# A new instruction order for the second and the steady groups of a graph-convolution kernel

## The reference, cut to what matters

```python
h0 = jnp.maximum(_layernorm(x, axis=-1), 0.0)          # rows of 1024
fv = h0.mean(axis=1)                                   # one value per node
nf = fv / norm(fv);  sim = nf[:, :, None] * nf[:, None, :]
_, idx = jax.lax.top_k(sim, 9);  idx = idx[..., 1:]    # 8 neighbours per node
adj = symmetric 0/1 matrix of them, diagonal 1         # 1024 x 1024 per batch
def _gc(x, adj, W, b):
    h = x @ W.T + b
    return einsum('bij,bjh->bih', adj / deg, h)
h = relu(_gc(h0.T, adj, W, b1));  h = _gc(h, adj, W, b2)
out = x + h.T                                          # W is the 256 x 256 input adj
```

## Time and profile before

| | |
|---|---|
| median of 3 runs | 477.64 us (476.87 to 478.04) |
| profiled execution | 475.69 us |
| its span, first to last instruction | 473.9 us |
| PE busy | 421.5 us (89%) |
| DVE busy | 395.6 us (83%) |
| ACT busy | 307.8 us (65%) |
| POOL busy | 220.9 us (47%) |
| mean granted clock of PE | 0.986 |

### The profile page before, as it was taken

How to read it: one execution, slowest core, us unless ns; L and a number is a source line. 1 busy time by engine, 2 the same in 40 slices (tenths; PEclk the granted TensorE clock), 3 DMA queues, 4 the chain that set the end, 5 groups by cost and what they waited for, 6 DMA issues and landing times.

```text
span 473.9 us, 7615 instructions
## 1 busy us (share of the span) xinstructions
PE 421.5 (89%) x2220; PEld 176.2 (37%) x2220; DVE 395.6 (83%) x682; ACT 307.8 (65%) x657; POOL 220.9 (47%) x937
## 2 busy tenths in 40 slices
PE   0653898999978799899999999899999999999996
PEld 0121343334323344344443443344434444344432
DVE  5999898988897998999899998999899828854463
ACT  2979687989766777667777769667766843014400
POOL 2536656374736435552737454744656253415200
PEclk9995999999999999999999999999999999999999
DMA  8990000159202493065703590078404400341026
GB/s 295 382 410 29 1 0 2 44 223 340 107 0 94 174 326 119 1 262 175 273 3 132 205 355 21 0 268 284 160 0 179 177 2 0 142 160 55 0 94 262
DMA packets 19401, 68.21 MB, mean 144 GB/s; under 512 B 1824, under 2 KB 2464, under 8 KB 19360
## 3 DMA queue, kind: packets, MB, share of 16 engines
q1 hardware_dynamic: 19360, 67.73, 38.2%
HBM read 34.17 MB, written 33.55 MB: 143 GB/s over the span
## 4 chain that ended last, share of the span: by engine, by line
DVE 39%; PE 31%; ACT 11%; issue 9%; POOL 7%; DMA 1%; POOLq 1%; SPq 0%; DVEq 0%; ACTq 0%
PE ps L451 26%; DVE hl L1109 9%; DVE hl L1118 7%; DVE bn L1087 7%; DVE xs L1134 5%; ACT hl L663 4%; ACT hf L654 4%; PE ps L457 3%; ACT hl L675 2%; DVE fv L1150 2%; DVE idx L1158 2%; POOL gat L876 2%; PE pm L506 1%; DMA xs<-x_dram 1%; POOL nw L858 1%
## 5 line engine op out<-in xcount | busy, mean ns | idle before, releaser
L451 PE MATMUL ps<-hl,wh 128*128 128x512 f16 x896 | 268.7, 382 | 20.6 <-DVE wl L1293 11.3
L451 PE MATMUL ps<-hl,wl 128*128 128x512 f16 x448 | 170.5, 381 | 0.0
L451 PEld LDWEIGHTS ps<-hl,wh 128*128 128x128 f16 x896 | 83.9, 99 | 131.4 <-issue 22.0
L654 ACT ACTIVATE hf<-xs,nbias,rstd 128x1024 f32<-128x1024 f32 x64 | 79.2, 1237 | 25.3 <-POOL nbias L862 17.4
L1109 DVE TENSOR_TENSOR hl<-hf,hl 128x1024 f16<-128x1024 f32 x64 | 76.9, 1211 | 15.5 <-ACT hl L663 15.3
L1134 DVE SCALAR_TENSOR_TENSOR xs<-ps,sc,xs 128x1024 f32<-128x1024 f32 (+1 forms) x71 | 78.9, 1137 | 5.9 <-PE ps L457 5.9
L1118 DVE SCALAR_TENSOR_TENSOR hl<-ps,hl 128x1024 f16<-128x1024 f32 (+1 forms) x55 | 57.2, 1083 | 20.3 <-ACT hl L675 20.2
L675 ACT ACTIVATE hl<-ps 128x512 f16<-128x512 f32 x96 | 55.7, 594 | 22.0 <-PE ps L457 22.0
L663 ACT ACTIVATE hl<-hf 128x1024 f16<-128x1024 f32 x64 | 67.6, 1056 | 2.0
L1087 DVE BATCH_NORM_STATS2 bn<-xs 128x6 f32<-128x512 f32 x96 | 61.2, 678 | 5.0 <-DMA xs<-x_dram 5.0
L451 PEld LDWEIGHTS ps<-hl,wl 128*128 128x128 f16 x448 | 44.0, 98 | 53.5 <-issue 1.1
(11 more groups left out here) (146 smaller groups left out, 537.6 us busy)
## 6 DMA issues: line engine op xcount, KB each, us to landing
xs<-x_dram SPq DMA_DIRECT2D x62, 512.0 KB, 7.4
out_dram<-xs SPq DMA_DIRECT2D x31, 1024.0 KB, 5.1
xs<-x_dram SPq DMA_DIRECT2D x4, 256.0 KB, 3.7
out_dram<-xs SPq DMA_DIRECT2D x4, 256.0 KB, 2.1
wt<-adj_t_dram SPq DMA_DIRECT2D x1, 256.0 KB, 9.8
b1r<-b_row_dram SPq DMA_DIRECT2D x1, 128.0 KB, 9.3
b2r<-b_row_dram SPq DMA_DIRECT2D x1, 128.0 KB, 10.8
cs<-consts_dram SPq DMA_DIRECT2D x1, 84.5 KB, 9.6
```

The lines of the kernel that those rows point to most:

```text
L451: pe.matmul(bank(i, e), w[:, k, o], src, start=(k == 0 and w is wh and part == 0), stop=False)
L654: act.activation(hf[:, c % NHF], xs[:, n % NX, k], ACT.Relu, bias=nbias[:, n % RB, k:k + 1], scale=rstd[:, n % RB, k:k + 1], accum_out=s_a ...
```

## The change

Only the order of instructions on PE, ACT and DVE changes; POOL's and SP's lists stay.

- PE: `class_sizes(2)` moves from behind unit 15 of group 1 to behind unit 0 of group 2, and `times_q1(2)` from behind `rows1` of units 0 and 1 to behind unit 2.
- ACT, group 1: `means_copy(2, 1)`, `y_hi` 6 and 7 and a root go ahead of both chunks of batch 12; `scalar_stats(15)` and the roots of 14 and 15 ahead of the chunks of 13; `class_count(2)` and `split_rows(4)` ahead of the first chunk of 14.
- ACT, steady groups: the first `y_hi` ahead of a root; the second chunk of FIRST+8 ahead of the root of FIRST+9; in group 2 `class_values` behind the first chunk of FIRST+8.
- DVE, group 1: the low part of batch 12 leaves the search and goes between the finals; the list behind is written anew, with `top_c` ahead of the row steps, and the low parts of 13 and 14 at its end.
- DVE, steady groups: `h_lo` of FIRST+8 ahead of `root_inverse` of FIRST+9; `y_lo` 6 ahead of `top_c`; the first `final` ahead of `h_lo` of FIRST+9, and `root_inverse` of FIRST+10 ahead of its second chunk.

```diff
@@ tensor @@
-                        if g == 1 and i == 0 and u == us[0]:
-                            class_sizes(1)
+                        if g in (1, 2) and i == 0 and u == us[0]:
+                            class_sizes(g)
+                        if g == 2 and i == 2 and u == us[2]:
+                            times_q1(g)
...
-                    if i == (2 if g < 2 else 0):
+                    if g != 2 and i == (2 if g < 2 else 0):
                         times_q1(g)
...
                         plain_rows(g + 1)
-                    else:
+                    elif g > 1:
                         class_sizes(g + 1)
@@ scalar @@
                     root(FIRST[g] + 8)
                     means_copy(g + 1, 0)
-                    n = front(g, 1)
-                    make_h(n, 0)
                     means_copy(g + 1, 1)
                     y_hi(*us[6][1:])
                     y_hi(*us[7][1:])
                     root(FIRST[g] + 9)
+                    n = front(g, 1)
+                    make_h(n, 0)
                     make_h(n, 1)
                 else:
+                    y_hi(*us[0][1:])
                     root(FIRST[g] + 8)
-                    y_hi(*us[0][1:])
                     y_hi(*us[1][1:])
-                    class_values(g)
+                    if g > 2:
+                        class_values(g)
                     n = front(g, 1)
                     make_h(n, 0)
+                    if g == 2:
+                        class_values(g)
                     y_hi(*us[2][1:])
                     y_hi(*us[3][1:])
                     if to:
                         means_copy(g + 1, 0)
+                    make_h(n, 1)
                     root(FIRST[g] + 9)
-                    make_h(n, 1)
...
                 if g == 1:
+                    scalar_stats(FIRST[g] + 11, 2 * g + 2)
+                    root(FIRST[g] + 10)
+                    root(FIRST[g] + 11)
                     n = front(g, 2)
                     make_h(n, 0)
                     make_h(n, 1)
-                root(FIRST[g] + 10)
-                scalar_stats(FIRST[g] + 11, 2 * g + 2)
-                root(FIRST[g] + 11)
+                else:
+                    root(FIRST[g] + 10)
+                    scalar_stats(FIRST[g] + 11, 2 * g + 2)
+                    root(FIRST[g] + 11)
                 n = front(g, 3)
-                make_h(n, 0)
+                if g > 1:
+                    make_h(n, 0)
                 if to:
                     class_count(g + 1)
                     split_rows(2 * (g + 1))
+                if g == 1:
+                    make_h(n, 0)
                 make_h(n, 1)
@@ vector @@
                     n = front(g, 1)
-                    h_lo(n, 0)
                     top_a(g + 1)
                     y_lo(*y[6])
                     y_lo(*y[7])
                     top_b(g + 1)
+                    top_c(g + 1)
                     root_inverse(first + 9)
...
                     stats(first + 10, 0)
+                    h_lo(n, 1)
                     root_inverse(first + 9)
-                    h_lo(n, 1)
                     y_lo(*y[4])
                     y_lo(*y[5])
                     if to:
                         top_a(g + 1)
                         top_b(g + 1)
+                    y_lo(*y[6])
+                    if to:
                         top_c(g + 1)
-                    y_lo(*y[6])
                     y_lo(*y[7])
...
                 if g == 1:
-                    top_c(g + 1)
                     top_d(g + 1)
                     final(*end[0])
+                    final(*end[1])
                     stats(first + 10, 1)
                     mean_var(first + 10)
-                    final(*end[1])
+                    h_lo(n, 0)
+                    final(*end[2])
                     h_lo(n, 1)
-                else:
-                    mean_var(first + 10)
+                    final(*end[3])
+                    root_inverse(first + 10)
+                    top_sums(g + 1)
+                    u_sums(g + 1)
+                    top_e(g + 1)
+                    kinds(g + 1)
+                    root_inverse(first + 11)
+                    final(*end[4])
+                    classes(g + 1)
+                    final(*end[5])
                     n = front(g, 2)
+                    rows_x(2 * (g + 1))
+                    class_counts(g + 1)
                     h_lo(n, 0)
-                    final(*end[0])
-                    final(*end[1])
+                    rows_t(2 * (g + 1))
                     h_lo(n, 1)
+                    rows_w(2 * (g + 1))
+                    n = front(g, 3)
+                    h_lo(n, 0)
+                    class_degrees(g + 1)
+                    inverse_degrees(g + 1)
+                    h_lo(n, 1)
+                    continue
+                mean_var(first + 10)
+                n = front(g, 2)
+                final(*end[0])
+                h_lo(n, 0)
+                final(*end[1])
                 root_inverse(first + 10)
+                h_lo(n, 1)
                 final(*end[2])
...
                 root_inverse(first + 11)
-                if g == 1:
-                    n = front(g, 2)
-                    h_lo(n, 0)
-                    h_lo(n, 1)
                 final(*end[4])
```

## The result

| | before | after |
|---|---|---|
| median | 477.25 us (4 runs, 475.47 to 478.04) | 471.83 us (4 runs, 471.75 to 471.89) |
| profiled execution | 475.69 us | 471.83 us |
| its span | 473.9 us | 470.0 us |

The new kernel is faster: ratio 0.9899, 95% interval 0.9877 to 0.9922, 5.4 us. The forecast was 473.1. In the two profiled executions the span is 3.9 us shorter. Functions stand lower in the new file: `final` is L1146 (before L1134), `y_lo` L1130 (L1118), `h_lo` L1121 (L1109), the rest shifts alike on DVE, and `h_chunk` is L656, `h_hi` L665, `y_hi` L677, the last coefficient step L874. PE's lines are unchanged.

The account below looks back on a forecast made before the run. DVE's chain with detours over ACT and POOL bounds groups 2 to 5, PE group 6. Gains in groups 1 and 2 and laps of 51.0 (28.9 + 22.1) take 4.5 off 475.69: 471.2, plus 1.95 gives 473.1 us; range 470.2 to 476.6.

Parts of the forecast that it names:

- T(1): Start of the times_q2 product (mark T) in group 1: forecast at 133.6 instead of 135.44.
- F to T: From start of final 14 (mark F) to start of the times_q2 product (T): 28.9 us steady, 31.1 in group 2.
- The hold: Group 2: the moved h_lo on DVE holds POOL's class_sums at u_nodes, 1.0 us.
- B9: Batch FIRST+9; its POOL coefficients were forecast at F+21.0 in steady groups, at 185.0 (F+23.2) in group 2.
- Most of its waiting only moves: PE, ready 5 us early, waits at unit 1 of group 2; the gain is DVE's 2.9 us.
- The steady lap: Groups 3 to 5, from one times_q2 product to the next: 51.0 us, against 51.65 on average before.
- T to F: Steady groups, from start of the times_q2 product to start of the next final 14: 22.1 us.
- The held step of POOL: B9's last coefficient step, held under h_lo in the old order: coefficients took 2.89 us, 1.97 without the hold.
- the 0.92 wait goes; what it can give is capped: Steady groups: PE's 0.92 us wait for y_lo of unit 6 goes; its gain is capped by the product waiting for POOL.
- The steady lap stays: First rival, 20%: new DVE waits of 0.6 and 0.9 replace the 1.46 us wait; laps 51.65, time 475.1.
- Slower: Rival, 7%: y_lo 4 and 5 hold POOL under B9's coefficients, 2.3 us late in groups 2 to 5; 482.3 us.
- PE bounds at once: Rival, 12%: group 2's classes cost no delay and laps are PE's 50.6; gain 7.9 us, time 469.7.

Follow-up runs that it names:

- Experiment 2: Changed kernel with ACT's and DVE's steady-group lists (groups 2 to 7) in their old order; group 1's lists, PE's list and late class_values(2) stay new: 473.55 us.
- the filler: Changed kernel with 19 matmuls with zero weights put into PE's long wait at unit 1 of group 2: 473.39 us.
- Experiments 6 to 8: Changed kernel with class_values(2) ahead of FIRST+8's first chunk on ACT; with 19 zero matmuls in PE's long wait; with both: 471.98, 473.39, 471.01 us.
- Experiment 4: Changed kernel with, in groups 2 to 7, h_lo of FIRST+9's first chunk again ahead of the first final on DVE: 471.96 us.
- Experiment 9: Changed kernel with, in groups 2 to 7, root_inverse of FIRST+8 and y_lo of units 0 and 1 ahead of FIRST+7's second h_lo: 469.94 us.
- experiment 3: Changed kernel with, in groups 2 to 7, FIRST+8's second chunk again behind FIRST+9's root on ACT, its h_lo behind FIRST+9's root_inverse on DVE: 474.86 us.
- experiment 5: Changed kernel with top_c again ahead of y_lo of unit 6 on DVE in groups 2 to 6: 473.96 us.
- experiments 9 and 11: Changed kernel with y_lo 0 and 1 ahead of the second h_lo; then also group 1's final 14 and 15 ahead of batch 14's low parts: 469.94, 468.94 us.
- experiments 2 to 12: Eleven follow-up kernels, each the changed kernel with one or more orders altered or zero matmuls added on PE: 467.90 to 474.86 us.

## Why the prediction was right, and where it was off

**Group 1 was right.** T(1) was to come 1.84 sooner and the lap T(0) to T(1) shrank by 1.87. DVE was to idle 0.4, 1.3 and 0.6 in this stretch; it idles 0.55, 1.26 and 0.54. F(2) was forecast for 161.8 and is 161.08 in an execution that began 0.5 sooner. Experiment 2 shows that this part stands alone.

**Group 2 came out right by its sum, and a cost was missing from it.** The wait at unit 1 was to be about 5 us and was 4.21. F to T was to be 31.1 and is 31.23, T(1) to T(2) 59.23 against a forecast of 59.3. The hold is there: the POOL step at 179.48 took 1.40 us, and it lies under the `h_lo` of DVE at 179.57, a subtraction with both inputs in SBUF. The Trainium skill (SBUF — State Buffer, "Who interferes with whom") says that such an instruction contends with a GpSimd instruction that reads SBUF, and this trace agrees, with 1.40 against 0.2 to 0.3 for the steps around it. B9's coefficients were to come at 185.0 and its chunk starts at 184.29, 0.2 sooner than that when both are counted from T(0). What the sum lacked: PE's clock fell in the long wait, and PE's `times_q1` came 2.6 us later than with the filler. It cost nothing in T(2), because B9's chunk ended (185.66 + 1.06 = 186.72, in ACT's rows) just when PE closed units 6 and 7 (`rows1`, 186.33 + 0.39 = 186.72). Experiments 6 to 8 show both chains: each alone gives 0 or 0.6, both 1.8. Experiment 4, with the clock low for a shorter time and T(1) to T(2) at the same 59.23, says the same. "Most of its waiting only moves" was right, and incomplete.

**The steady lap has the mis-sized term, F to T.** It was to be 28.9 and is 29.26; the lap was to be 51.0 and is 51.4. The parts that the term was made of hold. The reciprocal was to be at F+19.0 (18.98), the last coefficient step at 0.20 (0.19), the coefficients at F+21.0 (20.94), the chunk free of POOL, `y_hi` 6 to the product 5.55 (243.67 - 238.13 = 5.54). Only the start of `y_hi` 6 is late, 238.13 instead of F+23.3 = 237.7. The 0.32 us of idling in ACT's row, ended by PE, say that PE's rows were the last thing to come, not the chunk. PE was late by its wait for `y_lo` 0: its half unit from 221.07 was over at 221.07 + 1.29 = 222.36, and the next began at 223.14, so 0.78 was lost. In the kernel before, PE had lost 0.64 us for the first `final` and 0.92 for `y_lo` 6 by this place, and the wait was in no steady lap; in experiment 4, where 0.46 of it is back, it is gone too. The step that failed is this: the forecast followed DVE's chain to B9's chunk and took PE as ready when the chunk was. Three laps by 0.4 make 1.2 us, and by the common start T(6) is 1.2 later than forecast: 4.5 sooner was expected, 401.03 - 397.20 = 3.83 was found, of which 0.5 is the start. A steady lap was to gain 0.65 and gained 0.2. Experiment 9 takes this wait and 0.95 us of B9's chain away, and the lap drops to 50.8.

**T to F was right**: 22.1 forecast, 22.14 measured, with 0.51 idle ahead of `final` 0 where 0.6 was expected.

**The held step of POOL was no cost of the old lap.** The sum for the new order leaves the hold out, rightly. But the prediction also holds it against the first rival, as if it had cost the old lap something. In the earlier trace rows the held step ends at 237.11, and in the earlier trace rows B9's chunk starts at 238.47, without a wait: ACT was busy until then, as in experiment 3. The 0.92 us of the hold cost the old lap nothing. What the change saves is on ACT, where B9's chunk starts at F+20.98 instead of F+22.13. In the new order the coefficients are awaited (0.94 in ACT's row), so there a hold would cost something; no run has one at this place.

**Which edit gives what.** The pair of chunk and root is the lap's gain (experiment 3, 0.7 to 0.8 a lap), as argued, but through ACT's list and not through POOL. `y_lo` 6 ahead of `top_c` gives nothing (experiment 5); "the 0.92 wait goes; what it can give is capped" was right, and 0 is the cap. The order at `final` 0 saves PE's wait there and makes DVE idle: it costs 0.3 to 0.4 in each lap up to T(5) and saves 0.4 in the one behind, so it loses 0.6 in all (experiment 4).

**The rivals.** "The steady lap stays" is the nearest to what happened: laps are 51.41 on average where it said 51.65, the forecast 51.0. Its new waits are there in part, 0.51 of 0.6 ahead of `final` 0 and 0.38 of 0.9 ahead of `rows_x`. "Slower", a second hold, is shown false: the `y_lo` over B9's coefficients leave POOL's steps at 0.19. "PE bounds at once" was false for this kernel, and is what experiments 9 and 11 make of it.

**The median**, 471.83 against 473.1, is 1.3 better than forecast although the marks are worse, and that is luck. The marks gave 0.7 less than forecast, and 1.2 less without the early start. But the profiled execution of before was 1.95 below its median, that of after is at its median, so the 1.95 that the forecast carried over was not there. The 5.4 us of the medians are 3.9 of the profiled pair and 1.56 that the profiled execution of before lies under the later median of 477.25. Nor was the new median taken a second time, and it lies low: the median less T(1) to T(7) is 159.1 us for the changed kernel and 159.6 to 161.2 for the eleven others that share its lists up to T(1) (experiments 2 to 12). So of the 5.4 us only 1.9 + 1.5 = 3.4, those from T(0) to T(7), are shown to be the lists', and 1 us or so of the rest may be a low draw. With 1.95 on top of 471.83 the time would have been 473.8, in the range as well. What this spread of single executions comes from stays open; T(0) varies by 2.8 us between profiles.

## What to carry to other kernels

Where several engines run hand-written lists, cut the trace into laps at one mark and ask of each instruction on the path which releaser comes next once the first is early: a chain that frees 1.3 us pays only up to that one, here PE, late by a wait of 0.8. Ask the same of the old order: a step held for 0.9 us costs nothing when its reader comes 1.4 us later. Two chains that end together show themselves only when both are shortened, so test a repair of one with the other's as well, in a two by two. A wait in the busiest engine that looks free because others bound may be what the next edit runs into.

## What the runs showed of the hardware

- TensorE's granted clock after a short wait isn't a function of the wait's length alone: at the same place of the same list, 2.15 us left it at 1.00 and 2.12 us at 0.53 in the 3 us behind. The wait of 4.21 us was followed by 0.50 over 2.65 us and 0.67 over 4.22 us, during which a matmul pair took 1.01 instead of 0.60; in experiment 4 the same wait was followed by 0.57 and 0.87. With 19 matmuls that do nothing in 4.26 us of that wait it stayed at 1.00 (one profile).
- A DVE subtraction from SBUF held even a POOL step of 128 by 2 elements to its own end (0.19 became 1.13 in experiment 3, 0.20 became 1.12 in the earlier trace rows). The `y_lo` from 233.47 on, with an input in PSUM, left the same step, at 235.16, at 0.19. In experiment 3 the hold was off the path that set the lap.
